# GpSimd splits V one head ahead, and V is loaded two head steps ahead of its split

## The reference

```python
x = x + gru(initial_state=cond, inputs=x)          # 128 steps, one after another
# then a transformer block with modulation by cond, on the new x
x1 = layernorm(x) * (1 + scale1) + shift1
q, k, v = split(x1 @ qkv_w + qkv_b)                # 16 heads of 128
p = softmax(q @ k.T / sqrt(128))                   # for each sequence and head
y = x + gate1 * ((p @ v) @ out_w + out_b)
h = gelu((layernorm(y) * (1 + scale2) + shift2) @ ffn_w1 + ffn_b1)
out = x + y + gate2 * (h @ ffn_w2 + ffn_b2)
```

## Time and profile before

| | |
|---|---|
| time, median of 3 runs | 994.74 us (994.41 to 996.46) |
| time of the profiled execution | 991.13 us |
| span of the profiled execution | 989.3 us |
| TensorE busy | 793.4 us (80%) |
| VectorE / ScalarE / GpSimd busy | 508.3 / 483.5 / 289.5 us |
| mean granted TensorE clock | 0.905 |

### The profile page before, as it was taken

One profiled execution on the slowest core, in us unless ns is written; L12 is line 12 of the kernel. 1 busy time (PEld: TensorE's weight loads), 2 busy tenths in 40 slices (PEclk: granted clock), 3 DMA queues, 4 the chain that ended last, 5 costly groups with the idle time before them and its releaser, 6 DMA issues.

```text
span 989.3 us, 23647 instructions
## 1 busy us (share of the span) xinstructions
PE 793.4 (80%) x9324; PEld 539.1 (54%) x9324; DVE 508.3 (51%) x1423; ACT 483.5 (49%) x1621; POOL 289.5 (29%) x326
## 2 busy tenths in 40 slices
PE   6999999999997767677676757675766676768998
PEld 5789999989874433334343434343443344434445
DVE  5676666666664443343545533454533454533454
ACT  4455656555564444444543444453443453445553
POOL 1322222222223223332324332333333333433030
PEclk9799999999999889897988888888887988889999
DMA  5224434343334333223322222212231322121001
GB/s 180 77 88 121 131 99 131 91 125 93 92 87 106 76 64 64 55 53 64 55 53 60 49 49 58 65 43 64 44 64 43 63 45 64 44 64 27 22 22 43
DMA packets 116262, 70.17 MB, mean 71 GB/s; under 512 B 72075, under 2 KB 108087, under 8 KB 116151
## 3 DMA queue, kind: packets, MB, share of 16 engines
q1 hardware_dynamic: 115575, 67.09, 27.5%
q10 hardware_dynamic: 576, 1.57, 0.4%
HBM read 32.98 MB, written 18.87 MB: 52 GB/s over the span
## 4 chain that ended last, share of the span: by engine, by line
issue 39%; PE 35%; POOL 20%; DVE 2%; DMA 2%; ACT 1%; SPq 0%; POOLq 0%; DVEq 0%
PE bank L630 8%; POOL p_lo L487 7%; POOL v_lo L496 7%; PE bank L525 6%; PE bank L527 5%; PE bank L526 5%; PE bank L545 4%; PE bank L638 4%; POOL v_hi L494 3%; DMA pT_lo<-p_lo 1%; POOL xr L482 1%; PE bank L532 1%; DVE h_hi L1249 1%; POOL xr L475 1%; PE bank L597 1%
## 5 line engine op out<-in xcount | busy, mean ns | idle before, releaser
L525 PE MATMUL bank<-pT_hi,v_hi 128*128 128x128 f16 x256 | 57.1, 250 | 177.7 <-DMA pT_lo<-p_lo 177.7
L1319 DVE TENSOR_REDUCE mx<-bank 128x4 f32<-128x512 f32 x64 | 44.3, 692 | 293.3 <-PE bank L527 293.3
L487 POOL TENSOR_TENSOR p_lo<-prob,p_hi 128x512 f16<-128x512 f32 x64 | 74.1, 1157 | 294.1 <-DVE prob L1328 285.7
L525 PEld LDWEIGHTS bank<-pT_hi,v_hi 128*128 128x128 f16 x256 | 28.2, 110 | 208.3 <-DMA pT_lo<-p_lo 208.2
L1067 ACT ACTIVATE aT_hi<-bank,small 128x512 f16<-128x512 f32 x64 | 44.0, 687 | 199.0 <-PE bank L527 199.0
L1047 ACT ACTIVATE prob<-bank,nmx 128x128 f32<-128x128 f32 x256 | 90.7, 367 | 68.3 <-DVE nmx L1322 67.8
L630 PE MATMUL bank<-h_hi,whh_hi 128*128 128x16 f16 x1536 | 111.5, 174 | 6.4 <-DVE h_hi L1249 6.2
L525 PE MATMUL bank<-y_hi,w_hi 128*128 128x512 f16 x248 | 111.9, 451 | 0.0
L630 PE MATMUL bank<-h_hi,whh_lo 128*128 128x16 f16 x1536 | 108.8, 172 | 0.9 <-issue 0.9
L526 PE MATMUL bank<-y_hi,w_lo 128*128 128x512 f16 x248 | 109.5, 441 | 0.0
L527 PE MATMUL bank<-y_lo,w_hi 128*128 128x512 f16 x248 | 107.3, 433 | 0.0
(11 more groups left out here) (153 smaller groups left out, 2227.9 us busy)
## 6 DMA issues: line engine op xcount, KB each, us to landing
v_spill<-v_rows SPq DMA_DIRECT2D x32, 512.0 KB, 3.8
v_full<-v_spill SPq DMA_DIRECT2D x64, 256.0 KB, 2.9
stage<-in_weights SPq DMA_DIRECT2D x16, 640.0 KB, 4.1
x<-in_x SPq DMA_DIRECT2D x16, 128.0 KB, 4.1
out<-xr SPq DMA_DIRECT2D x3, 512.0 KB, 3.1
xr<-in_ada_r SPq DMA_DIRECT2D x1, 1024.0 KB, 7.5
pT_hi<-p_hi SPq DMA_TRANSPOSE x64, 2.9
pT_lo<-p_lo SPq DMA_TRANSPOSE x64, 2.4
```

Of the source, the lines that this page charges most:

```text
L487: gtt(p_lo[:, d % 2, :], flat_prob[d % 2], p_hi[:, d % 2, :], sub).then_inc(p_l, 1)
L525: mm(ps, w[0], a[0], start=start, stop=False, skip_group_check=True)
L1319: nc.vector.reduce_max(mx[:, :], bank[3][:, :].rearrange("p (j s) -> p j s", j=QUAD), AX.X).then_inc(s_mx, 1)
```

## The change

GpSimd's order is written anew: V of step 0 is split ahead of the loop, and pass `d` does `prob_low(d)` and then `value_split(d + 1)`. The wait on `s_pn` is gone. The extra pieces of layer norm and residual are looked up by `d` and no longer by `d + 2`; the two pieces that then fall past the loop's end follow behind it. On SyncE's queue V of step `d + 2` is loaded behind the transposes of step `d`; before it was V of step `d + 1`, behind the same transposes. No computation is added or removed.

```diff
             load_values(1)
-            turn(0)
-            for d in range(1, HEADS):
+            for d in range(HEADS):
                 turn(d)
-                if d < 3:
-                    store_values(NBL - 3 + d, 1)
-                if d + 1 == H // 2:
+                if d + 2 == H // 2:
                     for n in (NBL - 2, NBL - 1):
                         sp.wait_ge(v_out[n % 2][1], 16 * (NBL // 2))
-                if d + 1 < HEADS:
-                    load_values(d + 1)
+                if d + 2 < HEADS:
+                    load_values(d + 2)
+                if 0 < d < 3:
+                    store_values(NBL - 3 + d, 1)
...
+            value_split(0)
             for d in range(HEADS):
+                g, i = d // H, d % H
                 prob_low(d)
+                if d + 1 < HEADS:
+                    value_split(d + 1)
                 if d >= H and (d + 1) % H == VAR:
                     norm_rstd(d // H - 1)
-                value_split(d)
-                g, i = (d + 2) // H, (d + 2) % H
-                if d + 2 < HEADS:
-                    pool.wait_ge(s_pn, d + 3)
                 if g > 0 and i in REST:
                     bias_rest(g - 1, REST[i])
...
+            for k in range(KD):
+                norm_low(NG - 2, k)
             norm_rstd(NG - 1)
```

## The result

The changed kernel takes **759.13 us** (median of 4 runs, 757.81 to 760.32) against 995.6 us before (median of 4, 994.41 to 1000.5): a ratio of 0.7617 (95% interval 0.7588 to 0.7647), 24% faster. The forecast was 744 us with a range of 729 to 795.

What follows compares the result with a forecast made beforehand. It took `p_lo`'s wait on `s_pn` to close a loop of 9.59 us a step. `mx` of step 63 at 316.4 + 60 × 5.24 + 12 = 642.8 gave span 738.8, profiled execution 740.6, median 744 us; range 729 to 795.

Steps and rivals of the forecast that it cites:

- What bounds the kernel: In attention, GpSimd's `p_lo` waits on `s_pn` for VectorE's product, closing a loop through all engines: 9.59 us a step.
- The clock is a loss that hangs on the first: In attention the granted clock averages 0.85 behind TensorE's waits; with TensorE busy throughout, 0.98 or more.
- TensorE, 5.24 us a step: TensorE's matmuls per attention step at full clock: scores 0.67, attend 0.67, keys, projection and queries 3.90, if nothing is waited for.
- The transpose chain: `p_lo` and its transpose land at 8.7 to 9.3 us, attend comes at 9.8: 0.5 to 1.1 us to spare.
- V's load: V of step d+2 lands at 10.3 us of step d's scale, its split begins at 11.35: hidden by 1.0 us.
- The softmax chain: From `mx` to `key_low`, which the next scores need: there at 4.91 us, 5.01 with semaphore, 0.23 to spare against 5.24.
- the port's rival: `v_lo` on GpSimd meets VectorE's product at their port: 0.5 us onto the chain, 760 us, up to 799; chance 0.14.
- Steps 3 to 63: From `mx` of step 3 to `mx` of step 63: 60 steps of 5.24 us plus 12 us of extra work.
- what doesn't vanish: Extra work beside attention steps: layer-norm transposes 7.2, gates 2.2, residuals 1, GpSimd's pieces 1.6; sum 12 us, between 0 and 27.
- Start: `p_lo` of step 0 stands behind V's first split: `mx` of step 3 comes 2.4 us later, bounds 0 and 4.5.
- End: Behind `mx` of step 63: 100.0 us before, less 4 (between −6 and 0) as attend of step 62 loses its wait.
- The rival on V's load: V's load, split, `p_lo` and transpose close a loop over two steps; at a 20 us landing 1145 us; chance 0.02.

## Why the prediction was right

It was right in direction and cause, and 15 us too low. For the profiled execution it was 19.7 too low (740.6 against 760.32); the 3.6 us that it added for the distance of median and profile were not there, as the profiled execution was 1.2 above the median. That 759 lies within the forecast's own range of 729 to 761 is luck: the upper end stood for 27 us of extra work, and some 11 were measured. Its steps one by one:

- **What bounds the kernel** held. The wait on `s_pn` closed the loop: removing it alone gives 755.56, keeping it beside the rest of the change 998.13.
- **The clock is a loss that hangs on the first** held: the granted clock is 1.00 in attention, and the span's mean stays at 0.90 in the run that keeps the wait and is 0.98 or more in the change and in the run that only drops it. TensorE's busy time fell by 74.6 us.
- **TensorE, 5.24 us a step**: 5.22 to 5.23 in the first group's steps, once `nmx` isn't held.
- **The transpose chain** held: no matmul's wait is put down to it after the first attend.
- **V's load**, hidden by 1.0 us, held: with `nmx` on ScalarE its landing is 1.0 us ahead of the split in the median step. In the change it is 1.4.
- **The softmax chain is the step that failed.** It put `key_low` at 4.91 in every step, 0.23 us ahead of need, with `nmx` at the 0.17 that it has in the trace before. In the change 29 of 64 steps have it at over 0.9, and a held step is 0.73 us longer; every second step of the first group misses the 5.2 to 5.5 us that the prediction gave as its sign. This is the mechanism of the port's rival, met by another instruction than the one I priced: I looked at the product, 0.8 us behind the end of `v_lo`, and it stayed at 0.69 in 54 steps (up to 1.04 in the others, where an extra piece of GpSimd runs on). But `nmx` begins 0.72 us behind `mx` in the trace before (rows below), so at 1.59 of the layout, and `v_lo`, 1.15 us long and ended at 2.7, begins at about 1.55. The layout could not tell which of the two comes first, but it could tell that they meet. That the result is near the rival's 760 is luck as well: that price was 0.27 us in all of 60 steps, for the product. The Trainium skill, page "SBUF — State Buffer", section "Who interferes with whom", lists `tensor_scalar` among the operations that, where their operands meet the conditions for it, can take both of VectorE's ports and so exclude a GpSimd instruction whole, and `tensor_reduce` as one that never does so on this chip. The rows agree with both: `nmx` ended with `v_lo`, while `mx`, which reads PSUM, took 0.68 to 0.69 us in all 64 steps.
- **Steps 3 to 63**: forecast 60 x 5.24 + 12 = 326.4 us, measured 663.24 − 318.31 = 344.9. The 18.5 us between them are `nmx`: with it on ScalarE the same stretch is 641.89 − 317.70 = 324.2 us, 20.7 less. So **what doesn't vanish** (12 us) was sized well as a sum: 324.2 − 60 x 5.225 = 10.7; its four terms were not measured apart.
- **Start**: forecast 2.4 us, measured 26.04 − 22.76 = 3.3 between `mx` of step 0 and of step 3 (318.31 − 292.27 after, 314.03 − 291.27 before). The other 1.0 by which `mx` of step 3 is late is there at step 0 already. The forecast's cause is the right one: the first attend now waits 5.9 us for a `p_lo` that stands behind V's first load (`v_hi` at 302.75, attend at 308.21: 5.5 us, against 5.5 to 5.8 in the forecast), and the kernel that puts it ahead again wins 2.4 us.
- **End**: forecast 96.0 us behind `mx` of step 63, measured 95.3.
- The sum of the span is then 738.8 + 18.5 + 1.9 − 0.7 = 758.5 (1.9: `mx` of step 3 at 318.31 and not at 316.4).
- **The rival on V's load** named a loop of two steps that decides from a landing of 15 us on. The landing stayed at 2.9 in the median. The run with V loaded one ahead shows that such a loop is real where it closes in one step.

The rows from which these numbers come: of the kernel before `mx` of step 0, then `mx` and `nmx` of the step in the earlier trace rows; of the kernel after `mx` of steps 0, 3 and 63; of the one with `nmx` on ScalarE `mx` of steps 3 and 63.

```profile
291.27 0.68 DVE L1319 TENSOR_REDUCE mx<-bank 128x4 f32<-128x512 f32 x1
...
662.05 0.69 DVE L1319 TENSOR_REDUCE mx<-bank 128x4 f32<-128x512 f32 x1 [4.23 <-PE bank L527]
662.77 0.17 DVE L1322 TENSOR_SCALAR nmx<-mx 128x4 f32<-128x4 f32 x1
```

```profile
292.27 0.68 DVE L1320 TENSOR_REDUCE mx<-bank 128x4 f32<-128x512 f32 x1
...
318.31 0.69 DVE L1320 TENSOR_REDUCE mx<-bank 128x4 f32<-128x512 f32 x1 [1.48 <-PE bank L528]
...
663.24 0.69 DVE L1320 TENSOR_REDUCE mx<-bank 128x4 f32<-128x512 f32 x1 [0.97 <-PE bank L528]
```

```profile
317.70 0.69 DVE L1322 TENSOR_REDUCE mx<-bank 128x4 f32<-128x512 f32 x1 [1.48 <-PE bank L528]
...
641.89 0.69 DVE L1322 TENSOR_REDUCE mx<-bank 128x4 f32<-128x512 f32 x1 [0.97 <-PE bank L528]
```

## What to carry to other kernels

Where an engine waits in every step, look for which step's result it waits for, not only for whose: `p_lo` seemed to run beside its own `p_hi`, and that it was the `p_lo` of the step before was the whole case. When a wait that kept two engines apart goes, lay out all instructions of both on one time scale, the smallest too: here an instruction of 4 columns lost 1 us, what was left of the other engine's instruction, more than five times its own length. And a bound that has 0.2 us to spare in 5.2 is not hidden; either give it room (move the small instruction to another engine, or let the long one wait for it) or put it into the sum.

## What was not expected of the hardware

That a 0.04 us difference in the start of two instructions decides 0.96 us: at 329.48 against 329.52 GpSimd came first and VectorE's `nmx` took 1.14 us, at 335.66 against 335.49 VectorE came first and took 0.17, while `v_lo` took 1.16 both times. And that a stall of this kind settles, in the first group, into a rhythm of two steps, 5.96 and 5.23 us, in which each held step frees the next.

The traces also show how long such a stall is. In the profile after, 34 of the `nmx`, 10 of the products and 3 of the subtractions `hid_lo` began while a GpSimd instruction on a large tile had between 0.16 and 1.13 us left. Each took longer by what was left less 0.14 to 0.15 us, whatever its own length (0.17 or 0.69 us): so 1.12 left and 0.97 lost at 329.52, and 0.64 left and 0.50 lost in the earlier trace rows. Where 0.10 us or less was left, nothing was lost. GpSimd's `rstd`, which works on 4 columns, held nothing: in the run without the wait three `nmx` began with some 0.46 us of it left and took 0.17. It goes the other way too: in the kernel before a `v_lo` that began at 894.55, 0.10 us behind a `hid_lo`, took 1.59 us.
